# A gated delta rule decoder layer: output tile in two buffers, its transpose later, one ScalarE copy moved

## What is computed

```
mixed = silu(causal_conv1d(h @ w_qkv))        # 4 taps; q, k: 16 heads, v: 32 heads, of 128
q, k  = l2norm(q), l2norm(k)
St    = St * exp(g_t);  delta = (v_t - k_t St) * b_t          # per token, as chunks of 128
St    = St + k_t delta; o_t = q_t St
core  = o * rsqrt(mean(o*o) + eps) * norm_weight * silu(h @ w_z)
x     = x + core.reshape(B, S, 4096) @ w_out
```

## Time and profile before

| what | before |
|---|---|
| median of 3 runs | 3383.51 us (3382.04 to 3384.68) |
| the profiled execution: time, span | 3382.74 us, 3380.9 us |
| PE busy in the span | 3202.4 us (95%) |
| DVE, ACT, POOL busy | 2222.3, 1794.1, 1946.0 us (66%, 53%, 58%) |
| mean granted TensorE clock | 0.990 |
| mean busy share of the 16 DMA engines, SP's queue | 30.2% |

### The profile page before, as it was taken

One profiled execution on the slowest core, in us unless ns is written; L12 is line 12 of the kernel. 1 busy time (PEld: TensorE's weight loads), 2 busy tenths in 40 slices (PEclk: granted clock), 3 DMA queues, 4 the chain that ended last, 5 costly groups with the idle time before them and its releaser, 6 DMA issues. The chain is left out here.

```text
span 3380.9 us, 59978 instructions
## 1 busy us (share of the span) xinstructions
PE 3202.4 (95%) x20064; PEld 2087.9 (62%) x20064; DVE 2222.3 (66%) x3366; ACT 1794.1 (53%) x5623; POOL 1946.0 (58%) x1888
## 2 busy tenths in 40 slices
PE   5899999999999999999999999999988999999999
PEld 2567666766676667666766666666663444454444
DVE  6788888878888888888888887888840100024553
ACT  2466666666666666666666666666652000011232
POOL 2677777777777777777777777777740000011132
PEclk8999999999999999999999999999989999999999
DMA  3233333333333333333343333333325222211001
GB/s 100 58 91 92 92 85 86 92 87 86 80 101 89 86 84 95 90 80 85 91 98 87 80 90 93 89 80 92 101 70 196 75 100 87 99 38 63 0 13 38
DMA packets 469200, 282.30 MB, mean 83 GB/s; under 512 B 311808, under 2 KB 410240, under 8 KB 463360
## 3 DMA queue, kind: packets, MB, share of 16 engines
q1 hardware_dynamic: 467600, 271.39, 30.2%
q10 hardware_dynamic: 1296, 7.09, 0.5%
HBM read 173.17 MB, written 88.34 MB: 77 GB/s over the span
## 5 line engine op out<-in xcount | busy, mean ns | idle before, releaser
L762 PE MATMUL acc<-xT,wc 128*128 128x512 f32 x2048 | 937.0, 601 | 9.4 <-ACT d_kks L1230 7.4
L762 PEld LDWEIGHTS acc<-xT,wc 128*128 128x128 f32 x2048 | 370.8, 191 | 381.2 <-issue 380.7
L1019 DVE SCALAR_TENSOR_TENSOR d_conv<-acc,wc,d_conv 128x511 f32<-128x511 f32 (+2 forms) x768 | 566.2, 737 | 36.6 <-ACT d_conv L1182 25.2
L775 PE MATMUL acc<-wc,xT 128*128 128x256 f32 x2048 | 473.4, 384 | 0.0
L775 PEld LDWEIGHTS acc<-wc,xT 128*128 128x128 f32 x2048 | 379.1, 190 | 46.3
L1064 DVE CAST_PREDICATED d_zm<-cons,d_tz 128x512 f16<-128x512 int32 x384 | 265.4, 691 | 160.3 <-PE d_tz L807 153.6
L1057 DVE STREAM_TRANSPOSE d_em<-d_dm 128x1024 f16<-128x1024 f16 x256 | 314.8, 1230 | 40.8 <-ACT d_dm L1246 40.8
L1542 PE MATMUL acc<-t_area 128*128 128x512 f32 x768 | 332.5, 592 | 0.8 <-ACT t_area L1991 0.8
L2048 POOL TENSOR_SCALAR t_veps<-t_mv 128x1 f32<-128x1 f32 x32 | 9.7, 303 | 546.1 <-DVE t_mv L1787 546.1
L1246 ACT ACTIVATE d_dm<-acc 128x512 f16<-128x512 f32 x384 | 229.8, 598 | 121.8 <-PE acc L820 121.8
L1182 ACT ACTIVATE d_conv<-acc,wc 128x512 f32<-128x512 f32 x256 | 177.2, 692 | 219.8 <-PE acc L762 172.0
(11 more groups left out here) (224 smaller groups left out, 6979.2 us busy)
## 6 DMA issues: line engine op xcount, KB each, us to landing
d_decay<-decay_rows SPq DMA_DIRECT2D x64, 512.0 KB, 5.1
v_rows<-d_vb SPq DMA_DIRECT2D x256, 128.0 KB, 2.6
d_vn<-v_rows SPq DMA_DIRECT2D x64, 512.0 KB, 3.7
core_rows<-d_ob SPq DMA_DIRECT2D x1024, 32.0 KB, 1.7
t_area<-core_rows SPq DMA_DIRECT2D x30, 1024.0 KB, 4.8
wc<-in_w SPq DMA_DIRECT2D x96, 256.0 KB, 3.1
k_rows<-d_kf SPq DMA_DIRECT2D x256, 64.0 KB, 3.2
d_kn<-k_rows SPq DMA_DIRECT2D x64, 256.0 KB, 2.9
```

What stands on the lines that cost most here:

```text
L762: last = nc.tensor.matmul(bank(TILE[j])[:, :], wtile(j, k), xT[:, k, r % B * S:(r % B + 1) * S], start=k == 0, stop=k == KT - 1)
L775: last = nc.tensor.matmul(bank(f"z{j}")[:, i * GV * P:(i + 1) * GV * P].rearrange("p (h n) -> p h n", h=GV), xT[:, k, r % B * S + (2 * j + ...
L1019: nc.vector.scalar_tensor_tensor(c[:, d:S], bank(TILE[j])[:, 0:S - d], tap(j, KS - 1 - d), c[:, d:S], ALU.mult, ALU.add).then_inc(taps, 1)
```

## The change

- `oo` becomes two buffers, chosen by the parity of the unit. `first_output(s)` waits for the `flip_o` of two units before instead of one.
- VectorE's `flip_o(f)` moves from ahead of `residual(s, 1, h)` to behind `flip_d(m, 3)`. It also waits for the squares of the output, which now write into `ob`.
- The scratch tile `junk` shrinks. `k_square` writes its unused element-wise result into `kf`, and six of the eight `o_square` into `ob`, behind a wait for the stores of the unit before. `flip_k` waits for the squares of the unit before (`k_squares`) instead of the landing of its store.
- On ScalarE `copy_d(m, 3)` stands ahead of `copy_kk(n)`.
- SP's order, GpSimd's order and TensorE's order stay.

```diff
-        oo = sb("oo", [P, GV, NC, P])
-        junk, ... = sb("junk", [P, 3 * NC, P], BF16), ...
+        oo = many("oo", 2, [P, GV, NC, P])
+        junk, ... = sb("junk", [P, GV, P], BF16), ...
 def flip_k(n):
-                wait(dve, k_moved, at(back(n, 1), 80, 64))
+                wait(dve, k_squares, at(back(n, 1), NC, NC))
 def flip_o(s):
                 dve.wait_ge(gated, at(s, GV, GV))
                 wait(dve, stored, at(back(s, 1), STORES, STORES))
+                dve.wait_ge(o_squares, at(s, GV * NC, GV * NC))
 # VectorE's slot
                     level_z(m, 2)
-                if finish:
-                    flip_o(f)
                 if recur:
                     residual(s, 1, 0)
...
                     level_z(m, 4)
                     flip_d(m, 3)
+                if finish:
+                    flip_o(f)
                 if project:
                     convolve(n, 2, 1)
 def k_square(n):
-                squares(..., lambda c: junk[:, c, :].rearrange("p (a j) -> p a j", j=32), kss, k_squares)
+                squares(..., lambda c: kf[:, :, c, :], kss, k_squares)
 def first_output(s):
-                wait(act, o_flipped, count(s, 1))
+                wait(act, o_flipped, count(s, 2))
 def o_square(s, c, h):
+                if (c, h) in ((1, 0), (0, 1)):
+                    out = junk[:, h, :]
+                else:
+                    wait(act, stored, at(back(s, 1), STORES, STORES))
+                    out = ob[:, c, h * NC:(h + 1) * NC, :].rearrange("p b j -> p (b j)")
 # ScalarE's slot
+                if invert:
+                    copy_d(m, 3)
                 if project:
                     copy_kk(n)
-                if invert:
-                    copy_d(m, 3)
-                if project:
                     first_tap(n, 2)
```

More of the change, by code:

```diff
@@ L342, in delta_rule @@
         vb, ob = sb("vb", [P, NC, GV * NC, 32]), sb("ob", [P, NC, GV * NC, 32])
-        oo = sb("oo", [P, GV, NC, P])
-        junk, kqs, kks = sb("junk", [P, 3 * NC, P], BF16), sb("kqs", [P, S]), sb("kks", [P, S])
+        oo = many("oo", 2, [P, GV, NC, P])
+        junk, kqs, kks = sb("junk", [P, GV, P], BF16), sb("kqs", [P, S]), sb("kks", [P, S])
         kss, qss, rkt, rk = sb("kss", [P, NC]), sb("qss", [P, NC]), sb("rkt", [P, NC]), many("rk", 2, [P, 2, NC])
@@ L691, in o_gate @@
             def o_gate(s, h):
-                o = oo[:, h, :, :]
+                o = oo[s[1] % 2][:, h, :, :]
                 pool.wait_ge(o_scaled, at(s, GV * NC, h * NC + NC))
@@ L1048, in flip_o @@
                 wait(dve, stored, at(back(s, 1), STORES, STORES))
-                nc.vector.transpose(ob[:, :, :, :], oo[:, :, :, :].rearrange("p h c (a j) -> p a (h c) j", a=NC)).then_inc(o_flipped, 1)
+                dve.wait_ge(o_squares, at(s, GV * NC, GV * NC))
+                nc.vector.transpose(ob[:, :, :, :], oo[s[1] % 2][:, :, :, :].rearrange("p h c (a j) -> p a (h c) j", a=NC)).then_inc(o_flipped, 1)
             def flip_e0(m):
@@ L1089, in output @@
                 dve.wait_ge(oq_ready, at(s, 6, 2 * c))
-                nc.vector.tensor_tensor(oo[:, :, c, :], psb[:, 0:GV * P].rearrange("p (h d) -> p h d", h=GV),
+                nc.vector.tensor_tensor(oo[s[1] % 2][:, :, c, :], psb[:, 0:GV * P].rearrange("p (h d) -> p h d", h=GV),
                                         oq[:, :].rearrange("p (h d) -> p h d", h=GV), ALU.add).then_inc(o_ready, 1)
@@ L1206, in k_square @@
                 wait(act, k_squares, at(back(n, 1), NC, NC))
-                squares(lambda c: kn[n[1] % 2][:, :, c, :], lambda c: junk[:, c, :].rearrange("p (a j) -> p a j", j=32), kss, k_squares)
+                squares(lambda c: kn[n[1] % 2][:, :, c, :], lambda c: kf[:, :, c, :], kss, k_squares)
             def q_square(n):
@@ L1234, in o_scale @@
                 for c in range(NC):
-                    o = oo[:, h, c, :]
+                    o = oo[s[1] % 2][:, h, c, :]
                     nc.scalar.activation(o, o, ACT.Copy, scale=r2[:, h, c:c + 1]).then_inc(o_scaled, 1)
@@ L1271, in first_output @@
                 act.wait_ge(o_done, at(s, NC, 1))
-                wait(act, o_flipped, count(s, 1))
-                nc.scalar.activation(oo[:, :, 0, :], psb[:, 0:GV * P].rearrange("p (h d) -> p h d", h=GV), ACT.Copy).then_inc(first_ready, 1)
+                wait(act, o_flipped, count(s, 2))
+                nc.scalar.activation(oo[s[1] % 2][:, :, 0, :], psb[:, 0:GV * P].rearrange("p (h d) -> p h d", h=GV), ACT.Copy).then_inc(first_ready, 1)
             def o_square(s, c, h):
@@ L1280, in o_square @@
                     act.wait_ge(o_ready, at(s, NC - 1, c))
-                nc.scalar.activation(junk[:, NC + h * NC + c, :], oo[:, h, c, :], ACT.Square, scale=HD ** -0.5,
+                if (c, h) in ((1, 0), (0, 1)):
[3 more added lines that the diff above has]
+                    out = ob[:, c, h * NC:(h + 1) * NC, :].rearrange("p b j -> p (b j)")
+                nc.scalar.activation(out, oo[s[1] % 2][:, h, c, :], ACT.Square, scale=HD ** -0.5,
                                      accum_out=oss[:, h, c:c + 1]).then_inc(o_squares, 1)
@@ L1340, in slot @@
                     read_q(s, 1, 0)
-                if project:
-                    copy_kk(n)
                 if invert:
@@ L1345, in slot @@
                 if project:
+                    copy_kk(n)
                     first_tap(n, 2)
```

## The result

The changed kernel takes 3497.39 us (median of 4 runs, 3497.11 to 3501.5) against 3384.10 us before: ratio 1.0338, 95% interval 1.032 to 1.0356. That is 113 us slower; the prediction was 87 us slower, 3470 us, with a range to 3525.

The account below looks back on a forecast made before the run. TensorE, busy 95% of the span, was taken to set the slot, with two short waits. Slots without weight loads +17 us, r = 3 +20, r = 0 +54, ends -4: +87 on 3383.5 gives 3470 us, range 3395 to 3525.

Parts of the forecast that it names:

- The holes go, TensorE's own slot is shorter: TensorE: waits of 0.81 and 0.53 us vanish; slot 36.75 us instead of 37.65 if nothing new ends last.
- The transpose's move: VectorE: with two output buffers, residuals and first_output no longer wait for flip_o; worth 0.60 to 0.81 us a slot.
- priced as a gain: ScalarE: copy_d(m, 3) first removes the 0.53 us hole; both edits together start the query tile 0.9 us earlier.
- free slot: TensorE: slot with both edits when no new wait ends last, 36.75 us.
- The late transpose makes the queue late: SP's queue: flip_o ends 7.5 us later, delaying 16 stores and the loads behind them.
- The loop through the keys: k_square through flip_o and SP's queue to landed keys: 37.0 to 39.3 us, middle 38.2; 39.1 for r = 3.
- The taps: Slots r = 0: first_tap waits for taps issued behind the late stores; slots 41.4 us, +54 us in all.
- 5 to 7 us of idle time before the first tap: ScalarE, each new head: a sign that the forecast is right; before, this idle time was 3.17 us.
- 3.6 us later than before, all of it lost, +54 us: Slots r = 0: taps land 19.9 us after level_d(m, 2) instead of 16.3, delaying TensorE in 15 slots.

Follow-up runs that it names:

- e8: Changed kernel with stores one slot later, early taps in two buffers, and ScalarE's order as before the change (copy_kk ahead of copy_d(m, 3)): 3318.89 us, ratio 0.9804.
- e1: Kernel before with only ScalarE's order changed, copy_d(m, 3) ahead of copy_kk: 3394.16 us, ratio 1.0032.
- e7: Changed kernel with output stores issued one slot later and taps in two buffers loaded early, ScalarE's new order kept: 3337.22 us, ratio 0.986.
- e3: Changed kernel with flip_o back in its old place ahead of the residuals; buffers, squares and ScalarE's order as changed: 3393.98 us, ratio 1.0029.
- e4: Kernel before with one more wait on SP's queue: store_o waits until flip_d(m, 3) is done, engine orders untouched: 3486.48 us, ratio 1.0303.
- e5_taps_early: Changed kernel with convolution taps in two buffers by head, loaded ahead of store_o in slot r = 3: 3448.43 us, ratio 1.0194.
- e9_queue_late_taps: Kernel before with store_o waiting for flip_d(m, 3) and taps in two buffers loaded ahead of the store: 3417.84 us, ratio 1.0096.

## Why the prediction was right

- *The holes go, TensorE's own slot is shorter.* Right, at 36.65 to 36.95 us once the queue is out of the way, for 36.75 forecast. How the two edits share it was not right. The transpose's move was to give at most 0.81 us and gives 1.0 (37.65 to 36.65) without the ScalarE edit (e8). That edit, priced as a gain, costs 0.2 us a slot (e1), and 0.3 in the free slot (e7 against e8). The forecast saw the wait for bank 1; what `copy_kk` feeds on GpSimd, and VectorE's wait for it, it put at nothing without naming it.
- *The late transpose makes the queue late.* Right, and it is nearly all of the loss: e3 takes 103 us back, e4 makes 102 us by the queue alone. The two are not made up alike: in e4 the slots r = 0 have all but a little of it, in the changed kernel 81 us. The prediction held 16 issues (7.72 to 9.10 us) against one landing (1.7 us). One issue, 7.72 / 16 = 0.48 us, is shorter than its landing; it is 16 in a row that hold what stands behind them.
- *The loop through the keys.* Right in kind, a little long for r = 1 and 2 (38.06 and 37.77 for 38.2) and short for r = 3 (39.56 for 39.1). `load_k` kept its 6 us behind `load_decay` without the pause, as taken. The slots r = 1 and 2 cost 15 x (0.14 + 0.43) = 9 us less than forecast and those of r = 3 15 x 0.46 = 7 us more; that the two nearly cancel is luck.
- *The taps.* The wait was sized nearly right: 8.4 + 0.9 + 0.1 + 2.4 = 11.8 us from the end of `flip_o` to the first tap. Measured are 12.3 in the mean of the 15 (11.5 to 13.5); the slot shown, with 11.5, is among the shortest. The stores took the 8.4 us of the forecast in the mean; the 8 KB load landed in 2.8 us, not 2.4, nor the 1.7 of the earlier trace rows. The sign "5 to 7 us of idle time before the first tap" was missed: it is 8.2 us (122.4 / 15). By the ring order that the Trainium skill states ("DMA: Bandwidth & Descriptors", Queues, rings and completion order) the load lands behind the weight loads, and the trace agrees: issued some 0.5 us behind the second of them, it takes 2.8 us where those take 3.1.

```profile
wc<-in_w SPq DMA_DIRECT2D x96, 256.0 KB, 3.1
...
wc<-in_w SPq DMA_DIRECT2D x16, 8.0 KB, 2.8
```

- *The term that was too small* is "3.6 us later than before, all of it lost, +54 us": the slots r = 0 cost 5.40 us each, 81 us in all. 0.5 us of the difference is the later tap. The rest is the clock: the lost time was counted at full clock, and after the hole TensorE ran at half of it. In the slot shown it took 1.69 us from the first of the refining matmuls (1324.86) to the tile behind them (1326.55), and 4.72 us for the tile. The same place in the kernel before, in order of time:

```profile
1264.74 0.23 PE L841 MATMUL d_tz<-d_dm,d_bh 128*128 128x128 f16 x1
...
1265.64 3.65 PE L762 MATMUL acc<-xT,wc 128*128 128x512 f32 x8
```

There the refining matmuls take 0.90 us and the tile 3.65. The difference is 0.79 + 1.07 = 1.9 us in this slot. It is not the same in each: from the first refining matmul to the one behind the tile, the 15 slots take 5.80 us in the mean (4.86 to 7.16) where the kernel before takes 4.39. That is 1.4 us a slot, 21 us in all, and with 8 us for the later taps about what the forecast of these slots fell short by, 27 us, and the whole forecast by 26. The slots of r = 3 have it in part: in 6 of the 15 the clock fell. In one of them that took 41.36 us TensorE waited 2.92 us for `first_output`, and the clock was 0.60 in the four microseconds behind:

```profile
1614.00:1618.00 4.00, 1.07 (x14) 0.84 (x9) 0.00 (x0) 3.05 (x15) 1.57 (x2) 1.00 0.68 168
1618.00:1622.00 4.00, 4.00 (x32) 3.77 (x31) 2.33 (x4) 1.50 (x6) 1.71 (x3) 0.60 0.31 123
```

- *Left open.* The clock's share is read from rows at either level; no run held the clock up through the same hole. Which issue time the stores take, 7.7 or some 9 us, was not explained.

## What to carry to other kernels

An instruction that is moved takes its DMAs with it, and in an in-order queue everything behind them: count from its new end through the queue to the first engine that waits, as a loop of one period, before counting the hole that it leaves. When a move of this kind loses, move its transfer in the queue's order as well; here that one change was worth 150 us. Two late things behind one queue hide each other, so that taking away the longer one brings out the other and not the whole time. And an order that ends a wait on one engine sooner may hand a third engine its input later (here GpSimd, and through it VectorE); its sign can change with what sets the period.

## What was not expected of the hardware

TensorE's granted clock fell to 0.50, the lower of its two levels (1.2 GHz), in all the slots r = 0, where the engine had stood idle for 3.13 to 4.88 us; in the slot shown it was back at 1.00 in the stretch from 1332 us on. With idle times of 0.81 and 0.53 us, and of 0.77 and 2.27 us in the changed kernel, it stayed at 1.00. In e5_taps_early it fell in one slot around a wait of 1.77 us, so in these runs the length of one wait alone does not tell whether it falls. Where it fell in the slots r = 0, the wait cost more than its own length: 4.0 us of idle time in the mean and 1.4 us of slow matmuls behind it. And two DMAs that stand behind the same late queue do not add up: in e4_queue_late the slots that wait for the taps cost 6.7 us a head and the late keys hardly anything in the others, in e9_queue_late_taps the keys came out at 0.3 to 1.0 us a slot in r = 0 to 2.
